# Part of a weight transpose moved out of the first top-k search into an earlier FFN and kept in DRAM; the search's remaining transposes spread evenly; a weighted sum with its operands exchanged

## The chip, the cores and the metric

One core of one Trainium2 chip. The metric is device microseconds of one execution. The engines are PE (TensorE), DVE (VectorE), ACT (ScalarE), POOL (GpSimd) and SP (SyncE), which issues all the DMAs of this kernel.

## The reference

x is 8 x 112 x 256 in float32, the context 8 x 375 x 256. Four layers follow each other, each of the form x = x + tanh(gate) * f(x):

```
x += tanh(g0) * dtw_align(ctx, layernorm(x))           # dynamic time warping, backtracked
x += tanh(f0) * bit_linear(silu(dwconv(bit_linear(layernorm(x), w1))), w2)      # the FFN
x += tanh(g1) * attention(layernorm(x), ctx)           # 16 heads of 16
x += tanh(f1) * neuron_ffn(layernorm(x))
# neuron_ffn(x):
a0 = mean_s(gelu(x @ input_patterns.T))                # 8 x 2048
repr = a0 where a0 is among its row's 256 largest, else 0
a1 = gelu(repr @ process_input_weights.T)              # 8 x 1024, weights 1024 x 2048
w  = softmax(the row's 128 largest of a1);  agg = w @ process_values[chosen]    # 8 x 128
a2 = gelu(agg @ output_input_weights.T)                # 8 x 2048
out = (the row's 256 largest of a2) @ output_patterns[chosen]     # 8 x 256, the same for all s
```

## The kernel before

The whole problem lives on one core. Every engine has one hand-written instruction list. `plan_psum` (L88) deals out the eight PSUM banks in the order in which PE fills them; `claim` (L477) makes PE wait until the bank's last content was drained, `fill` and `drain` count on two semaphores of the bank.

**The FFN** (from about 205 us) works on eight tiles c of 128 hidden units and two halves of 448 tokens. PE: `ffn_up(c, half)` (L1926, product at L1931). DVE: `dequantise` (L1092), then the conv's last tap at L1116 and, each second c, a maximum at L1123 to L1128. ACT: loop L1594 to L1607 (middle tap L1600, left tap L1603, Silu of tile c - 2 at L1607). POOL adds the left tap (L777). The tile buffers `hb` and `ct0` have three slots, so tile c waits for the conv of c - 3. After the loop the scale is transposed and spread (`hmaxT`, `s2bc`, L1957 to L1968), DVE scales and rounds eight tiles, ACT rounds three of them (L1610 to L1614), and PE makes `ffn_down` (L1969 to L1981), whose tile c waits for its rounding. In the FFN SP loads the attention's key stacks (`load_stack`, L593) for batch entries 0, 1, 2 into the three slots of `ks`, and stores and loads split keys (L606, L599). The attention starts at about 284 us, on the first slot.

**The last layer**. PE makes 32 pattern products (L2087) up to about 477 us; beside them SP loads `piw`, two slots of one 128 x 2048 tile of the process weights each (L645 to L648). Then comes a search for the 256 largest of each row (`largest`, L1289): the values lie as 128 lanes of 128, and in each of 2 x 8 rounds DVE counts how many lie below three candidates (L1343), PE adds the counts of a row's lanes (`count`, L2174 to L2186), DVE compares them (L1355) and makes the next candidates (L1361). Into this search the transposes of the process weights are placed (L2206 to L2217): PE does four groups of four 128 x 128 transposes (L2213) for tile i, then two counts, for i = 0 to 7; ACT copies each group from PSUM to `piwT` (L1718). After the ties (L2194, L2195) DVE makes the picked values, PE transposes them (L2203), DVE copies them to `repr32` (L1393), and PE, after 32 waits for the drains of all the groups (L2221 to L2223), starts `process` (L2230).

The second search has 12 rounds of 7 candidates, DVE and ACT sharing the counting. Its result goes to the weighted sum `aggr` (L2256, L2259): for each of 8 tiles the 128 x 128 process values stand as PE's weights and 8 columns of softmax terms pass; then, for the sum of the terms, a matrix of ones stands as weights. DVE takes the reciprocal (L1418) and multiplies (L1420), and PE makes `output` (L2267). A third search, the final product and the write follow.

Of the kernel before, what the change touches and what calls it, by code (L numbers as in the profile page):

```python
# [20 lines left out]
NH, HD = 16, 16  # L21
# [9 lines left out]
UP0 = 3  # L31
ACT_ROUNDS = (1, 3, 5)
# [55 lines left out]
def plan_psum():  # L88
# [42 lines left out]
    for b in range(B):  # L131
        ring(("expand", b))
    for half in range(2):
        for h in range(DH):
            ring(("qxT", h, half))
        ring(("sxbc", half))
        if half == 0:
            for c in range(UP0):
                ring(("ffn_up", c, 0))
    for c in range(HT):  # L140
        for half in range(0 if c >= UP0 else 1, 2):
            ring(("ffn_up", c, half))
    for half in range(2):
        ring(("hmaxT", half))
    p.add("s2bc", 6, 7)
    for pair in range(HB):
        p.add(("ffn_down", pair), pair)
# [35 lines left out]
    for p_ in range(NPT):  # L183
        for m in range(NIT // 4):
            ring(("piwT", p_, m), (0, 1, 2, 3))
    for k in range(3):
# [12 lines left out]
        elif k == 1:  # L199
            p.add("aggr", 2)  # L200
            p.add("output", 3)
# [7 lines left out]
def build_program(nc, x_in, ctx_in, g_xattn, g_ffn, w1_in, conv_w, conv_b, w2_in,  # L209
                  wq_in, bq_in, wk_in, bk_in, wv_in, bv_in, wo_in, bo_in,  # L210
                  pat_in, piw_in, pval_in, oiw_in, opat_in, out, key_parts, keys):
    plan = plan_psum()
    ctx = ExitStack()
    with ctx:
# [81 lines left out]
        last_stack = rk.at - 2 * NH * SC  # L296
        ln0 = Region(rk.at).take("ln0", [S, B, D])
# [131 lines left out]
        agr = r1.take("agr", [128, B])  # L429
# [73 lines left out]

        parts_stored = [sem(f"parts_stored{i}") for i in range(2)]
# [48 lines left out]
        def _(sp):  # L553
# [64 lines left out]
            for b in range(2):  # L618
                store_parts(b)
                load_keys(b + 2)  # L620
            sp.wait_ge(x_ready, B)
            sp.wait_ge(consts_ready, 1)
            for b in range(3):
                sp.dma_start(ks[SR:SR + 3, b, :, :], onesb[0:3, :].unsqueeze(1).broadcast_to([3, NH, SC])
                             ).then_inc(loaded["ones_k"], 16)
            for b in range(2):
                load_stack(b)
            for b in range(2, B):
# [3 lines left out]
                if b == 2:  # L632
                    load_stack(2)
# [11 lines left out]
            for i in range(NPT):  # L645
                if i >= 2:
                    wait_filled(sp, ("piwT", i - 2, NIT // 4 - 1))
                sp.dma_start(piw[:, i % 2, :], piw_in[128 * i:128 * (i + 1), :]).then_inc(loaded[f"piw{i % 2}"], 16)  # L648
# [140 lines left out]
        def _(dve):  # L789
# [644 lines left out]
        def _(act):  # L1434
# [158 lines left out]
            whole_columns(1)  # L1593
            for c in range(HT + 2):  # L1594
# [119 lines left out]
            for i in range(NPT):  # L1714
# [28 lines left out]
        def _(pe):  # L1743
# [191 lines left out]
            for half in range(2):  # L1935
# [32 lines left out]
            fill(ins, "s2bc")  # L1968
            for c in range(HT):  # L1969
# [236 lines left out]
            for i in range(NPT):  # L2206
                pe.wait_ge(loaded[f"piw{i % 2}"], 16 * (i // 2 + 1))
                for m in range(NIT // 4):
                    nm = ("piwT", i, m)
                    claim(pe, nm)  # L2210
                    for e in range(4):
                        c = 4 * m + e
                        ins = tr(bank(nm)[:, 128 * e:128 * e + 128], piw[:, i % 2, 128 * c:128 * c + 128],  # L2213
                                 ident[:, :])
                    fill(ins, nm)
                for r in (2 * i, 2 * i + 1):
                    count(0, r)  # L2217
            ties(0)
            sel_transpose(0)
            wait_drained(pe, ("selT", 0))  # L2220
            for i in range(NPT):  # L2221
                for m in range(NIT // 4):
# [90 lines left out]
```

## Time and profile before

| | |
|---|---|
| three executions | 618.41, 618.11, 621.31 us (median 618.41) |
| the profiled execution | 620.62 us; its span from the first to the last instruction 618.8 us |
| busy | PE 67%, DVE 69%, ACT 46%, POOL 16% |
| mean granted TensorE clock | 0.796 of full speed |

The profile gives for each instruction its line, engine, operands, start and duration, and in square brackets the idle time of its engine before it with what ended it. The granted clock of PE has two levels, 0.50 (1.2 GHz) and 1.00 (2.4 GHz). The chain of waits follows the work that ended last back from the last instruction.

### The profile page before, as it was taken

What the parts mean: (1) busy time and instruction counts of PE and PEld (TensorE: products, weight loads), DVE (VectorE), ACT (ScalarE), POOL (GpSimd) and SP (SyncE); (2) the same over time, 40 slices, a digit from 0 to 9 for tenths busy, and PEclk for the clock granted to TensorE, in tenths of its full rate; (3) what the DMA queues carried; (4) which work ended last, traced back from release to release, by engine and by line L of the source; (5) the groups of instructions that cost most, each with busy time, mean ns of one, the idle gap of its engine ahead of it and who ended that gap; (6) DMA issues with size and microseconds to landing.
All of it is one profiled execution on the core that took longest, in us unless ns stands there. A gap on an engine that the chain in (4) does not pass through costs nothing.

```text
span 618.8 us, 10227 instructions
## 1 busy us (share of the span) xinstructions
PE 415.4 (67%) x3424; PEld 295.1 (48%) x3424; DVE 428.8 (69%) x1711; ACT 284.9 (46%) x657; POOL 97.9 (16%) x235
## 2 busy tenths in 40 slices
PE   3798899732293601856899998999999556207206
PEld 3467686511172301834677776776455552107203
DVE  7645999899938697768788887864534763671673
ACT  3745444812224773444365556654434451450440
POOL 6780000000065462035700000000000000000000
PEclk9997699755576855669699999999999887755556
DMA  9600004194025980000566857600300560000002
GB/s 283 187 1 1 1 2 150 57 210 107 2 78 104 139 141 19 0 0 15 147 116 89 200 82 139 173 1 1 137 1 0 176 234 0 2 1 0 0 1 60
DMA packets 34666, 47.23 MB, mean 76 GB/s; under 512 B 5542, under 2 KB 32055, under 8 KB 32823
## 3 DMA queue, kind: packets, MB, share of 16 engines
q1 hardware_dynamic: 34614, 46.58, 32.2%
q8 instruction: 28, 0.46, 0.3%
q14 instruction: 24, 0.19, 0.1%
HBM read 37.87 MB, written 8.60 MB: 75 GB/s over the span
## 4 chain that ended last, share of the span: by engine, by line
PE 54%; DVE 24%; ACT 11%; issue 6%; POOL 4%; DVEq 0%; POOLq 0%; ACTq 0%
PE ps L2087 7%; PE ps L2041 4%; DVE PR L1028 4%; PE ps L2028 4%; ACT below L1708 4%; PE ps L2017 4%; PE ps L1850 4%; PE ps L1858 3%; PE ps L2003 3%; PE ps L2213 2%; PE ps L1914 2%; DVE prod L1024 2%; DVE below L1343 2%; PE ps L1809 2%; DVE ct L1116 2%
## 5 line engine op out<-in xcount | busy, mean ns | idle before, releaser
L1679 ACT ACTIVATE E<-ps 125x448 f32<-125x448 f32 x96 | 52.1, 543 | 46.3 <-PE ps L2028 46.2
L1215 DVE TENSOR_REDUCE negm<-ps 112x1 f32<-112x375 f32 x128 | 66.0, 544 | 10.6 <-PE ps L2017 7.4
L2186 PE MATMUL ps<-cnt,same 128*128 128x3 bf16 (+4 forms) x40 | 6.8, 170 | 61.6 <-ACT below L1708 41.1
L2017 PE MATMUL ps<-ks,qs 96*112 96x375 bf16 x128 | 44.2, 357 | 2.8 <-ACT qs L1672 2.5
L2041 PE MATMUL ps<-E,v 125*32 125x112 f32 x768 | 42.7, 273 | 0.0
L2028 PE MATMUL ps<-qs,ks 99*125 99x112 bf16 x384 | 40.4, 229 | 1.0 <-ACT E L1679 0.5
L1203 DVE TENSOR_REDUCE acts<-gel 128x4 f32<-128x448 f32 x32 | 19.8, 620 | 29.3 <-ACT gel L1647 29.3
L2028 PEld LDWEIGHTS ps<-qs,ks 99*125 99x125 bf16 x384 | 35.2, 141 | 9.7 <-issue 6.3
L2186 PEld LDWEIGHTS ps<-cnt,same 128*128 128x128 bf16 (+1 forms) x40 | 4.3, 107 | 64.7 <-issue 64.7
L1647 ACT ACTIVATE gel<-ps 128x448 f32<-128x448 f32 x32 | 17.3, 543 | 29.3 <-PE ps L2087 29.3
L1236 DVE CAST qs<-ps 3x448 bf16<-3x448 f32 x32 | 20.1, 630 | 13.4 <-PE ps L2058 13.3
L762 POOL CAST kp<-kx 128x750 bf16<-128x750 f32 x8 | 6.5, 810 | 141.1 <-ACT path L1565 127.7
L1028 DVE TENSOR_TENSOR_SCAN PR<-UU,PR,prod 128x94 bf16<-128x94 bf16 x63 | 26.1, 414 | 2.2
L2003 PE MATMUL ps<-qp,pick 128*96 128x112 bf16 x384 | 25.5, 218 | 2.2 <-issue 2.2
L2003 PEld LDWEIGHTS ps<-qp,pick 128*96 128x96 bf16 x384 | 24.8, 128 | 4.3 <-issue 3.0
L2087 PE MATMUL ps<-ln3Ta,patT 128*128 128x448 f32 x64 | 25.3, 543 | 1.2 <-ACT gel L1647 1.2
L1718 ACT ACTIVATE piwT<-ps 128x512 f32<-128x512 f32 x32 | 17.1, 603 | 16.4 <-PE ps L2213 16.3
L1888 PE MATMUL ps<-lanes_at,turned 64*47 64x32 bf16 x125 | 5.2, 203 | 28.4 <-ACT turned L1557 28.4
L2087 PE MATMUL ps<-ln3Tb,patT 128*128 128x448 f32 x64 | 24.2, 539 | 0.0
L1672 ACT ACTIVATE qs<-ps 96x448 bf16<-96x448 f32 x32 | 17.2, 539 | 14.4 <-PE ps L2003 14.4
L2041 PEld LDWEIGHTS ps<-E,v 125*32 125x32 f32 x768 | 19.6, 109 | 8.5 <-issue 5.5
L2017 PEld LDWEIGHTS ps<-ks,qs 96*112 96x112 bf16 x128 | 16.7, 134 | 14.1 <-issue 8.9
(371 smaller groups left out, 1131.3 us busy)
## 6 DMA issues: line engine op xcount, KB each, us to landing
ks<-key_parts SPq DMA_DIRECT2D x48, 187.5 KB, 6.8
piw<-fn_process_input_weights SPq DMA_DIRECT2D x8, 1024.0 KB, 4.9
key_parts<-kp SPq DMA_DIRECT2D x48, 93.8 KB
ctx_again<-in_ctx SPq DMA_DIRECT2D x7, 512.0 KB
keys<-kx SPq DMA_DIRECT2D x16, 187.5 KB, 2.1
kx<-keys SPq DMA_DIRECT2D x8, 375.0 KB, 6.7
ctxP<-in_ctx SPq DMA_DIRECT2D x8, 256.0 KB, 6.2
patn<-in_L_ffn_input_patterns SPq DMA_DIRECT2D x1, 2048.0 KB, 16.1
```

What stands on the lines that cost most here:

```text
L1028: dve.tensor_tensor_scan(PR[:, t, 2:PW], UU[:, t, 0:2 * RB], prod[:, :], PR[:, t, 1:2], ALU.mult, ALU.add).then_inc(traced, 1)
L1203: dve.tensor_reduce(a0[:, HB * half:HB * half + HB, i % NIT], gel[:, i % 2, :].rearrange("p (b s) -> p b s", b=HB), AX.X, ALU.add).then_in ...
L1215: drain(dve.tensor_reduce(negm[:, n:n + 1], bank(nm)[0:S, 0:SC], AX.X, ALU.max, negate=True), nm)
L1236: drain(dve.tensor_copy(qs[SR:SR + 3, (f + 1) // 4 % 3, n:n + 4, :].rearrange("p n s -> p (n s)"), bank(nm)[SR:SR + 3, 0:4 * S]), nm)
L1679: drain(fn(E[:, (KCH * f + c) % 6, :], bank(nm)[0:KC, 0:4 * S], ACT.Exp), nm)
L1708: ins = fn(below[0:n, m, :], val[0:n, :], ACT.Sign, bias=cand[0:n, m:m + 1], scale=-1.0, accum_out=cnt[0:n, m:m + 1])
L1850: ins = mm(bank(nm)[0:KC, 0:D], ctxT[:, h, b, KC * c:KC * c + KC], wvT[:, h, :], start=(h == 0), stop=(h == DH - 1))
L2003: ins = mm(bank(nm)[0:SR, S * i:S * i + S], pick[:, part, 4 * (u % 2) + i, :], qp[:, tile, part, S * (u // 4):S * (u // 4) + S], start=(pa ...
L2017: fill(mm(bank(nm)[0:S, 0:SC], qs[0:SR, u // 4 % 3, n, :], ks[0:SR, u // 4 % 3, n, :], start=True, stop=True), nm)
L2028: ins = mm(bank(nm)[0:KC, S * i:S * i + S], ks[0:SR + 3, f // 4 % 3, n, KC * c:KC * c + KC], qs[0:SR + 3, f // 4 % 3, n, :], start=True, s ...
L2041: ins = mm(bank(("pv", b))[32 * g:32 * g + 32, S * t:S * t + S], v1[:, c, b, (HD + 1) * n:(HD + 1) * n + 32], E[:, (KCH * f + c) % 6, S * ...
L2087: ins = mm(bank(nm)[:, 0:448], patT[:, h, 128 * (i % NIT):128 * (i % NIT) + 128], ln3T[i // NIT][:, h, :], start=(h == 0), stop=(h == DH - 1))
```

## The change

Process-weight tiles 0, 1, 2 (of 8) are transposed in the FFN. Six blocks of 128 x 1024 (`piwE`, e = 0 to 5) are loaded to `piw_raw` (3 slots), transposed by PE (8 transposes into two banks), copied by ACT to `piw_out` (2 slots) and stored by SP to a new DRAM tensor `piw_t`. Their buffers lie in slots 1 and 2 of `ks`, whose loads come later. The FFN's ring of banks has six banks, not eight. In the last layer three DMAs bring the 3 MB back (`load_turned`), and the search holds the 20 groups of the other five tiles: three ahead of it, then one after nearly each count. The waits for the groups' drains stand ahead of the transpose of the picked values. The weighted sum has the softmax terms (8 columns) as weights and the values (128 columns) and one column of ones pass; its 8 x 128 result is scaled, transposed by PE and copied by DVE.

```diff
@@ plan_psum
+    six = tuple(range(6))
+    n[0] = 0
     for half in range(2):
         for h in range(DH):
-            ring(("qxT", h, half))
+            ring(("qxT", h, half), six)
...
+    for e in range(2 * NE - 1):
+        p.add(("piwE", e), 6, 7)
...
     p.add("s2bc", 6, 7)
+    p.add(("piwE", 2 * NE - 1), 4, 5)
@@ SP, ahead of and in the FFN
-            for b in range(3):
-                (ones of slot b)
-            for b in range(2):
-                load_stack(b)
-            for b in range(2, B):
+            load_ones(0)
+            load_stack(0)
+            for e in range(3):
+                load_raw(e)
+            store_parts(2)
+            load_keys(4)
+            store_parts(3)
+            load_keys(5)
+            for e in range(2 * NE):
+                if e + 3 < 2 * NE:
+                    wait_filled(sp, ("piwE", e))
+                    load_raw(e + 3)
+                wait_drained(sp, ("piwE", e))
+                sp.dma_start(piw_t[8 * (e % 2):8 * (e % 2) + 8, :, 128 * (e // 2):128 * (e // 2) + 128
+                                   ].rearrange("c n p -> n c p"), piw_out[:, e % 2, :, :]
+                             ).then_inc(turned_stored[e % 2], 16)
+            for i in range(2):
+                sp.wait_ge(turned_stored[i], 16 * NE)
+            for b in range(1, 3):
+                load_ones(b)
+            for b in range(1, 3):
+                load_stack(b)
+            for b in range(4, B):
@@ SP, last layer
+            load_turned(0, 5)
+            load_turned(12, NIT)
+            for i in range(NE, NPT):
+                j = i - NE
+                if j == 2:
+                    wait_filled(sp, ("pattern", 2 * NIT - 1))
+                    load_turned(5, 12)
+                if j >= 2:
                     wait_filled(sp, ("piwT", i - 2, NIT // 4 - 1))
+                sp.dma_start(piw[:, j % 2, :], piw_in[128 * i:128 * (i + 1), :]).then_inc(loaded[f"piw{j % 2}"], 16)
@@ ACT, in the FFN's loop over c (after the Silu of c - 2) and after it
+            def keep_turned(e, at):
+                nm = ("piwE", e)
+                wait_filled(act, nm)
+                if e >= 2:
+                    act.wait_ge(turned_stored[e % 2], 16 * (e // 2))
+                drain(fn(piw_out[:, e % 2, :, :]..., psum[:, at:at + 2, :], ACT.Copy), nm)
...
+                if 0 <= c - 3 < 2 * NE - 1:
+                    keep_turned(c - 3, 6)
             load_table(ACT.Sqrt)
+            keep_turned(2 * NE - 1, 4)
@@ PE, in the FFN
+            def early_turn(e, at):
+                nm = ("piwE", e)
+                claim(pe, nm)
+                pe.wait_ge(raw_loaded[e % 3], 16 * (e // 3 + 1))
+                for k in range(8):
+                    ins = tr(psum[:, at + k // 4, 128 * (k % 4):128 * (k % 4) + 128],
+                             piw_raw[:, e % 3, 128 * k:128 * k + 128], ident[:, :])
+                fill(ins, nm)
             for c in range(HT):
                 for half in range(0 if c >= UP0 else 1, 2):
                     ffn_up(c, half)
+                if 0 <= c - 3 < 2 * NE - 1:
+                    early_turn(c - 3, 6)
...
             fill(ins, "s2bc")
+            early_turn(2 * NE - 1, 4)
@@ PE, first search
+            turns = (NPT - NE) * (NIT // 4)
+            lead = 3
+            for g in range(lead):
+                turn_weights(g)
+            for r in range(2 * ROUNDS[0]):
+                count(0, r)
+                share = [lead + (turns - lead) * q // (2 * ROUNDS[0]) for q in (r, r + 1)]
+                for g in range(*share):
+                    turn_weights(g)
+            ties(0)
+            pe.wait_ge(turned_loaded, 48)
+            for i in range(NE, NPT):
                 for m in range(NIT // 4):
+                    wait_drained(pe, ("piwT", i, m))
             sel_transpose(0)
             wait_drained(pe, ("selT", 0))
-            for i in range(NPT):
-                for m in range(NIT // 4):
-                    wait_drained(pe, ("piwT", i, m))
@@ PE, weighted sum (the waits for pval and oiwT now stand ahead of sel_transpose(1))
             for i in range(NPT):
-                mm(bank("aggr")[:, 0:B], pval[:, i, :], cells(esel, NPT)[:, :, i], start=(i == 0),
-                   stop=(i == NPT - 1))
-            for i in range(NPT):
-                ins = mm(bank("aggr")[:, B:2 * B], ones[:, :], cells(esel, NPT)[:, :, i], start=(i == 0),
+                mm(bank("aggr")[0:B, 0:DPV], cells(esel, NPT)[:, :, i], pval[:, i, :], start=(i == 0), stop=False)
+                ins = mm(bank("aggr")[0:B, DPV:DPV + 1], cells(esel, NPT)[:, :, i], ones[:, 0:1], start=False,
                          stop=(i == NPT - 1))
             fill(ins, "aggr")
+            claim(pe, "aggT")
+            wait_drained(pe, "aggr")
+            fill(tr(bank("aggT")[:, 0:B], agg8[:, :], ident[0:B, 0:B]), "aggT")
@@ DVE, weighted sum
-            did(dve.reciprocal(agr[:, :], bank("aggr")[:, B:2 * B]))
+            did(dve.reciprocal(agr[:, :], bank("aggr")[0:B, DPV:DPV + 1]))
             settle()
-            drain(tt(agg[:, :], bank("aggr")[:, 0:B], agr[:, :], ALU.mult), "aggr")
+            drain(ts(agg8[:, :], bank("aggr")[0:B, 0:DPV], agr[:, 0:1], None, ALU.mult), "aggr")
+            wait_filled(dve, "aggT")
+            drain(dve.tensor_copy(agg[:, :], bank("aggT")[:, 0:B]), "aggT")
```

## Rows read from the trace of the kernel before

**Rows 1.** The page's chain that ended last, shares of the span by engine.
```profile
PE 54%; DVE 24%; ACT 11%; issue 6%; POOL 4%; DVEq 0%; POOLq 0%; ACTq 0%
```
**Rows 2.** Timeline of DVE, first search: start us, us, engine line, [idle before <- releaser].
```profile
485.22 0.16 DVE L1355 SCALAR_TENSOR_TENSOR reached<-ps,most 128x3 f32<-128x3 f32 x1 [0.21 <-PE ps L2186]
...
488.50 0.16 DVE L1355 SCALAR_TENSOR_TENSOR reached<-ps,most 128x3 f32<-128x3 f32 x1 [1.78 <-PE ps L2186]
...
492.14 0.16 DVE L1355 SCALAR_TENSOR_TENSOR reached<-ps,most 128x3 f32<-128x3 f32 x1 [0.43 <-PE ps L2186]
...
505.35 0.16 DVE L1355 SCALAR_TENSOR_TENSOR reached<-ps,most 128x3 f32<-128x3 f32 x1 [1.99 <-PE ps L2186]
```
**Rows 3.** Timeline of PE, first search.
```profile
490.13 1.94 PE L2213 MATMUL ps<-ident,piw 128*128 128x128 f32 x16
...
501.78 3.49 PE L2213 MATMUL ps<-ident,piw 128*128 128x128 f32 x16
...
515.67 0.16 PE L2194 MATMUL ps<-tie,same 128*128 128x1 bf16 x1 [1.37 <-DVE eq L1372]
```
**Rows 4.** Timeline of DVE and PE, from the picked values to the process product.
```profile
517.81 0.29 DVE L1393 COPY repr<-ps 128x128 f32<-128x128 f32 x1 [0.63 <-PE ps L2203]
...
519.25 8.44 PE L2230 MATMUL ps<-piwT,repr 128*32 128x512 f32 x64 [1.48 <-issue]
```
**Rows 5.** Windows: busy of PE, PEld, DVE, ACT, POOL, then granted clock, DMA share, GB/s.
```profile
195.00:213.00 18.00, 10.80 (x60) 7.16 (x60) 11.28 (x28) 12.06 (x20) 3.71 (x3) 0.73 0.97 130
...
488.00:500.00 12.00, 6.76 (x59) 5.96 (x57) 8.96 (x68) 7.11 (x14) 0.00 (x0) 1.00 0.73 262
519.00:522.40 3.40, 3.15 (x20) 0.97 (x24) 0.00 (x0) 0.00 (x0) 0.00 (x0) 0.55 0.00 0
522.40:528.00 5.60, 5.60 (x55) 1.82 (x48) 0.00 (x0) 0.85 (x2) 0.00 (x0) 1.00 0.00 0
560.00:576.00 16.00, 14.62 (x66) 14.14 (x66) 0.59 (x3) 0.37 (x2) 0.00 (x0) 0.50 0.00 0
```
**Rows 6.** Timeline of PE and DVE at the weighted sum, and one PE transpose ahead of it.
```profile
530.20 0.27 PE L2243 MATMUL ps<-ident,pmx 128*8 128x128 f32 x1 [1.07 <-DVE pmx L1403]
...
558.67 0.18 PE L2194 MATMUL ps<-tie,same 64*64 64x1 bf16 x1 [1.34 <-DVE eq L1372]
558.72 0.19 PE L2195 MATMUL ps<-tie,under 64*64 64x1 bf16 x1
...
560.71 3.55 PE L2256 MATMUL ps<-esel,pval 128*128 128x8 f32 x16 [0.36 <-DVE esel L1416]
...
567.71 0.21 DVE L1418 RECIPROCAL agr<-ps 128x8 f32<-128x8 f32 x1 [7.10 <-PE ps L2259]
...
568.22 6.97 PE L2267 MATMUL ps<-agg,oiwT 128*128 128x8 f32 x32 [0.55 <-issue]
```
**Rows 7.** Timeline of ACT, FFN loop; one row of ACT's copies in the first search.
```profile
224.26 1.14 ACT L1600 ACTIVATE ct<-hb,cb,cws 128x896 f32<-128x896 f32 x1 [2.11 <-DVE hb L1099]
...
239.19 0.95 ACT L1607 ACTIVATE hs<-ct 128x896 f32<-128x896 f32 x1 [3.46 <-DVE ct L1116]
...
502.90 0.60 ACT L1718 ACTIVATE piwT<-ps 128x512 f32<-128x512 f32 x1 [2.75 <-PE ps L2213]
```
**Rows 8.** Timeline of PE and ACT, FFN: products in the loop, then the rounding.
```profile
215.28 1.68 PE L1931 MATMUL ps<-qxT,w1T 128*128 128x448 bf16 x4 [5.42 <-DVE hb L1099]
...
252.76 1.04 ACT L1612 ACTIVATE hs<-hs,magic 128x896 f32<-128x896 f32 x1 [11.11 <-DVE hs L1160]
...
253.32 10.06 PE L1978 MATMUL ps<-w2T,q 128*112 128x256 bf16 x64 [2.71 <-DVE q L1156]
```
**Rows 9.** The page's DMA issues: out<-in, count, KB each, median us from issue to landing.
```profile
ks<-key_parts SPq DMA_DIRECT2D x48, 187.5 KB, 6.8
piw<-fn_process_input_weights SPq DMA_DIRECT2D x8, 1024.0 KB, 4.9
...
pval<-in_L_ffn_process_values SPq DMA_DIRECT2D x1, 512.0 KB, 16.7
```

More of the change, by code:

```diff
@@ L31 @@
 UP0 = 3
+NE = 3
 ACT_ROUNDS = (1, 3, 5)
@@ L132, in plan_psum @@
         ring(("expand", b))
+    six = tuple(range(6))
+    n[0] = 0
     for half in range(2):
         for h in range(DH):
-            ring(("qxT", h, half))
-        ring(("sxbc", half))
+            ring(("qxT", h, half), six)
+        ring(("sxbc", half), six)
         if half == 0:
             for c in range(UP0):
-                ring(("ffn_up", c, 0))
+                ring(("ffn_up", c, 0), six)
+    for e in range(2 * NE - 1):
+        p.add(("piwE", e), 6, 7)
     for c in range(HT):
         for half in range(0 if c >= UP0 else 1, 2):
-            ring(("ffn_up", c, half))
+            ring(("ffn_up", c, half), six)
     for half in range(2):
-        ring(("hmaxT", half))
+        ring(("hmaxT", half), six)
     p.add("s2bc", 6, 7)
+    p.add(("piwE", 2 * NE - 1), 4, 5)
     for pair in range(HB):
@@ L182, in plan_psum @@
     n[0] = 0
-    for p_ in range(NPT):
+    for p_ in range(NE, NPT):
         for m in range(NIT // 4):
@@ L210, in build_program @@
                   wq_in, bq_in, wk_in, bk_in, wv_in, bv_in, wo_in, bo_in,
-                  pat_in, piw_in, pval_in, oiw_in, opat_in, out, key_parts, keys):
+                  pat_in, piw_in, pval_in, oiw_in, opat_in, out, key_parts, keys, piw_t):
     plan = plan_psum()
@@ L296, in build_program @@
         last_stack = rk.at - 2 * NH * SC
+        early_raw = Region(rw.at + 2 * NH * SC)
+        piw_raw = early_raw.take("piw_raw", [128, 3, 1024])
+        piw_out = early_raw.take("piw_out", [128, 2, 8, 128])
+        assert early_raw.at <= rk.at
         ln0 = Region(rk.at).take("ln0", [S, B, D])
@@ L428, in build_program @@
         pmd = r1.take("pmd", [B, B])
-        agr = r1.take("agr", [128, B])
+        agr = r1.take("agr", [B, 1])
+        agg8 = r1.take("agg8", [B, DPV])
         agg = r1.take("agg", [128, B])
@@ L502, in build_program @@
              "pmx_ready pmd_ready pexp_ready vec scl pol").split()]
+        raw_loaded = [sem(f"raw_loaded{i}") for i in range(3)]
+        turned_stored = [sem(f"turned_stored{i}") for i in range(2)]
+        turned_loaded = sem("turned_loaded")
         parts_stored = [sem(f"parts_stored{i}") for i in range(2)]
@@ L2205, in _, with turn_weights @@
             act_transpose(0)
-            for i in range(NPT):
-                pe.wait_ge(loaded[f"piw{i % 2}"], 16 * (i // 2 + 1))
-                for m in range(NIT // 4):
[L2209 to L2218, printed above, removed]
+            def turn_weights(g):
+                i, m = NE + g // (NIT // 4), g % (NIT // 4)
+                pe.wait_ge(loaded[f"piw{(i - NE) % 2}"], 16 * ((i - NE) // 2 + 1))
+                nm = ("piwT", i, m)
+                claim(pe, nm)
+                for e in range(4):
+                    c = 4 * m + e
+                    ins = tr(bank(nm)[:, 128 * e:128 * e + 128], piw[:, (i - NE) % 2, 128 * c:128 * c + 128],
+                             ident[:, :])
+                fill(ins, nm)
+            turns = (NPT - NE) * (NIT // 4)
[9 more added lines that the diff above has]
+            pe.wait_ge(turned_loaded, 48)
+            for i in range(NE, NPT):
+                for m in range(NIT // 4):
+                    wait_drained(pe, ("piwT", i, m))
             sel_transpose(0)
             wait_drained(pe, ("selT", 0))
-            for i in range(NPT):
-                for m in range(NIT // 4):
-                    wait_drained(pe, ("piwT", i, m))
             for h in range(2):
@@ L2250, in _ @@
             ties(1)
+            pe.wait_ge(loaded["pval"], 16)
+            for m in range(NOT // 4):
+                wait_drained(pe, ("oiwT", m))
             sel_transpose(1)
```

26 lines of the change are left out of this document (15 added, 11 removed).

## The prediction

> **What bounds the kernel now.** I read the chain of waits first, for which engine sets the end, then the timelines of the stretches that the change touches, then the granted clock there. No engine bounds the kernel: the chain passes from PE (54%) to DVE (24%) to ACT (11%) [rows 1], so each edit is worth what it takes off the chain of its own stretch, and the profile's busy shares say little.
>
> In the first search the chain is DVE's: a round is three counts on DVE, a short PE matmul, a comparison and new candidates. Between the rounds' starts lie 1.71 us where nothing is in the way (483.98 to 485.69 in the timeline), with DVE idle for 0.21 us while PE counts [rows 2]. But every second count stands on PE behind 16 transposes. At the full clock they take 1.94 us, which is longer than the 1.5 us that DVE leaves PE, and DVE waits 0.43 us, not 0.21; at the half clock they take 3.29 us (not shown) or 3.49 us [rows 3], and DVE waits 1.78 and 1.99 us [rows 2]. That is what the even spreading goes for. The reader should then see 1.48 us of "issue" on PE after DVE has long copied the picked values: 32 semaphore waits [rows 4].
>
> In the weighted sum PE is all there is: from 560.71 to 567.67 it passes 8 columns over 128-column weights, 32 times, at the half clock [rows 5, 6]. In the FFN loop no engine is full; ACT has pauses of 2.11 and 3.46 us (and one of 1.36 us at 231.84), PE one of 5.42 us before it has even reached the last products [rows 7, 8].
>
> **The change, part by part.**
>
> *Search, spreading.* A group is four transposes: 0.49 us at the full clock (1.94 / 4), 0.87 us at the half clock (3.49 / 4) [rows 3]. One group after a count fits into DVE's 1.5 us at either clock. What goes is all that DVE waited above 0.21 us: 1.57 + 1.78, and four times 0.22 [rows 2], together **-4.2 us**. Nothing else is late in its place: ACT copies a group in 0.60 us [rows 7]; the load of tile 5 starts after the fourth group, some 8 us ahead of its first transpose, and a load lands in 4.9 us [rows 9], as do tiles 6 and 7 with some 3 us to spare. In the last round there are two groups: at the half clock 1.74 us, where PE has 1.37 us before the ties [rows 3]: **+0.35 us**, nothing at the full clock. I take the half clock, because PE has less to do than before; both earlier drops came beside pauses of PE.
>
> *Search, waits.* DVE's copy ends at 518.10, PE starts at 519.25 [rows 4], 1.15 us later; I leave 0.1 us of that for the hand-over itself. The 21 waits that are left (20 groups, and the returned tiles) pass in 0.7 us (1.05 / 32 each) between the ties and the picked values, which lie 1.65 us apart in the timeline (515.67 to 517.32). **-1.05 us.**
>
> *Loads of the returned 3 MB.* The first two start at 436.8, with 40 us of pattern products ahead of them; the third, 1.4 MB, starts at 477.9 and is wanted at 513. At the 262 GB/s of this stage [rows 5] it takes 5.4 us. No cost, with 30 us of cover.
>
> *Process stage, clock.* The clock is at the half level when the product starts and at the full from 522.40, 3.15 us later [rows 4, 5]. In ffn_down PE is dense from 253.32 and its 64 passes of 256 columns take 10.06 us [rows 8]; at 0.213 us each they would take 13.6, at the full clock half, so the last 3.6 us ran at the full clock and the rise came some 6 us after the start. If the product had to wait as long, it would lose half of the 2.9 us between. I take **+0.5 us**, a third of the way, with 0 and +1.4 as ends.
>
> *Weighted sum.* Before: 6.96 us to 567.67 for 32 passes [rows 6], 0.22 each, set by the load of 128 float32 columns. After: 16 passes of 128 columns over 8-column weights and 16 of one column. A float32 pass of 128 columns takes 0.22 us at the half clock (3.49 / 16 [rows 3]); the two tie matmuls, one column each with their weights changed between them, start 0.05 us apart [rows 6]. So 16 x 0.22 + 16 x 0.05 = 4.3 us, **-2.65 us**; above, if each small one costs as much as a full one, nothing is gained; below, 3.5 us. Added: a PE transpose of the 8 x 128 result, 0.27 us alone [rows 6] and 0.2 us of handing over, and a DVE copy with its hand-over, 0.3 us; DVE's product has 128 columns and not 8, 0.05 us: **+0.8 us**. The five waits moved ahead of the transpose of the picked terms: **-0.1 us**.
>
> The Trainium skill, "TensorE: Matmul & The Clock Gate", Part 3, says that a weight load overlaps running matmuls only in another row group. All weights here use all rows. But 16 transposes with a weight load each, all in the same rows, pass in 1.94 us at 0.12 us each [rows 3]; loads of 0.11 us and passes of 0.12 us one after the other would be 3.7 us. The trace speaks against the rule; it is one of the rivals.
>
> *FFN loop.* ACT gets five copies of 1024 columns. A 512-column copy takes 0.60 us, an 896-column Silu 0.95 [rows 7]: 1.05 us on that line. I laid the loop out with these durations (ACT 1.13, 0.95, 0.93 a tile; DVE 0.54 for a half tile, 1.05 for the conv, 2.05 and 1.08 for a maximum; POOL 2.0 and never beside DVE's two-input operations, as 211.45 in the timeline shows, where the conv took 3.02 and not 1.14 us). Before and after differ by **1.05 us**: four copies fall into ACT's pauses, and one shows, as PE's tile 6 comes 1.3 us late behind the third block (226.2 and not 224.9). PE cannot turn block e before ACT has kept block e - 1, and tile e + 4 stands behind it; this is the new wait, and DVE waits for it. At the ends: 0 if PE's clock is high and pauses suffice, 5.3 if nothing is covered.
>
> *After the loop.* The sixth block is turned from 250.6 to 252.3, in PE's pause of 2.71 us [rows 8], and kept by ACT to 253.4; ACT's first rounding started at 252.76 and is two times 1.04 us [rows 8], so PE's second tile of ffn_down has to wait until 255.6 and not 255.05: **+0.55 us**. PE is what bounds ffn_down (64 passes in 10.06 us), so it stays.
>
> *SP and DMA in the FFN.* The first slot's six loads come in 1.125 MB; at the 130 GB/s of a full queue [rows 5] they are in at about 203, block 0 behind them at about 206. PE wants it at 208 and could wait until 214 before tile 4 is late (its pause of 5.42 us [rows 8]). Blocks 3 to 5 are asked for two tiles ahead, and 512 KB is half of what lands in 4.9 us [rows 9]. ACT's third copy needs the first store landed: issued at 220, wanted at 227. SP stands in its waits until about 257, then loads slots 1 and 2 (2.25 MB, 17 us at 130 GB/s) to about 277; slot 1 is read at about 293. Behind SP's waits nothing is queued that is wanted before POOL's keys at 290. No cost; the cover is 15 us for slot 1.
>
> **The sum**: -4.2 + 0.35 - 1.05 + 0.5 - 2.65 + 0.8 - 0.1 + 1.05 + 0.55 = -4.75 us. The profiled execution took 620.6 us, the median is 618.4, so this is 615.9 against its own time and **613.7 us** against the median.
>
> **The rivals.**
>
> *A, the FFN covers nothing.* All six copies (6.3 us) and the late rounding show: instead of +1.6 it is +6.3, and the time is 618.4. Against it are 7 us of ACT's pauses; for it, that the pauses are where ACT waits for DVE, and DVE would then wait for PE. 0.11.
>
> *B, slower: the ring of stores.* Block e + 2 can be kept only when store e has landed. Two such periods lie between the first copy and the fifth, 17 us in the layout. A store of 512-byte rows might land as late as the 512 KB of 512-byte rows of pval did, 16.7 us [rows 9]; two of them are 33 us, and the FFN takes 16 us longer: 629. It decides from about 11 us a store on (2 x 11 - 17 = the 5 us gained). For it is that the rows are as short; against it, that pval stood behind 2 MB of another load and these stand behind 0.5 MB. 0.04.
>
> *C, the sum's passes gain nothing.* If each weight load waits for the pass ahead of it, each of the 16 wide passes costs as one alone, 0.27 us [rows 6], and each load and small pass 0.18: 7.2 us and not 4.3, and the stage is 1 us slower than before. Time 616.6. 0.07. It is the rule quoted above.
>
> *D, a clock gift.* The sum's wide passes bring PE to the full clock: `output` takes 6.97 us at the half clock [rows 6], and at the full one half of that; 3.4 us less, 610.3. Against it: PE was over 90% busy from 560 to 576 and stayed at 0.50 [rows 5], though with 8 columns a pass; and the sum is but 4.3 us long. 0.10. That transposes keep the clock up here is plain: from 488 to 500 PE did nothing but transposes and 3-column counts, and was granted 1.00 [rows 5].
>
> The same page, Part 4, says that in transpose mode the full clock does not engage. The trace disagrees, as that row shows. By the rule the search would run at the half clock, which costs the 0.35 us that the sum already holds.
>
> **The numbers.** Forecast 0.68, A 0.11, B 0.04, C 0.07, D 0.10. The range: below, the gifts of D less part of the costs; above, C, or a FFN with half of A: 610.5 to 617.2. About 0.5% (3.1 us) is what a measurement of this kernel tells from no change. Faster by more needs under 615.3: nearly all of the forecast and D, so 0.78. Within: the forecast's upper tail, C, A, so 0.17. Slower: 0.05.
>
> **What the profile should show.** DVE idle before L1355 0.21 us in all rounds of the first search, its rounds 28.3 us together and not 32.6; PE's process product 0.1 us behind DVE's copy; the sum 4.3 us from first pass to last; the stretch from the FFN loop's first product (205.5) to the maximum's transposes (243.4) 1 us longer than its 37.9; ffn_down's second tile waiting for ACT. The forecast fails if the FFN has grown by over 3 us, if PE waits for a raw block or ACT for a store, if slots 1 or 2 of the key stacks are late at 293 us, or if the sum's passes are 0.4 us each.

## The result, and where the time went

In paired runs on one chip the changed kernel takes 612.5 us (611.3 to 612.9, 4 runs) and the kernel before 619.9 (618.1 to 621.5, 4 runs): a ratio of 0.986, 95% interval 0.982 to 0.990. Run again (`after_again`), 612.1 against 620.0, 0.986 (0.982 to 0.990). The forecast was 613.7 us, in a range of 610.5 to 617.2, with 0.78 on faster.

The sum said -4.75 us, and the paired medians differ by 7.4 us. The forecast's 613.7 comes near to 612.5 in part because it starts from a median of 618.4 us, where the paired median of the kernel before is 619.9. The profiled executions differ by 7.7 us (620.6 and 612.9; spans 618.8 and 611.0). So the sum was right in sign and range, and not in each term. These are lines of the page of the kernel after: its busy times, its chain by engine and its DMA issues.

```profile
PE 420.8 (69%) x3425; PEld 291.9 (48%) x3425; DVE 430.6 (70%) x1712; ACT 284.7 (47%) x651; POOL 95.6 (16%) x235
...
PE 51%; DVE 25%; ACT 13%; issue 6%; POOL 4%; DVEq 0%; ACTq 0%; POOLq 0%
...
piw<-fn_process_input_weights SPq DMA_DIRECT2D x5, 1024.0 KB, 5.1
...
piw_raw<-fn_process_input_weights SPq DMA_DIRECT2D x6, 512.0 KB, 8.3
piw_t<-piw_out SPq DMA_DIRECT2D x6, 512.0 KB, 3.2
```

The chain still passes between engines, as in [rows 1], so the time must be read stage by stage. A stage here runs from the start of one instruction on the chain to the start of the next, in the timelines. Two executions of each kernel are shown (`before_again` is the kernel before, unchanged).

| stage, us | before | before_again | after | after_again |
|---|---|---|---|---|
| start to the FFN loop's first product | 205.54 | 204.42 | 204.89 | 204.86 |
| to the maximum's transposes | 37.85 | 37.68 | 40.49 | 40.41 |
| to ffn_down (two stages) | 9.93 | 9.93 | 9.93 | 9.93 |
| ffn_down to DVE's first x | 9.44 | 9.24 | 8.94 | 9.48 |
| x to the attention's first product | 21.40 | 21.31 | 21.97 | 21.44 |
| to the first search | 198.10 | 196.99 | 197.48 | 197.13 |
| first search to the transpose of picked values | 35.06 | 35.98 | 31.21 | 31.21 |
| that transpose to the process product | 1.93 | 1.93 | 0.83 | 0.83 |
| process product to its last transposes | 9.24 | 9.28 | 10.62 | 10.53 |
| second search | 32.22 | 32.27 | 32.26 | 32.29 |
| weighted sum to the output product | 7.51 | 7.51 | 5.12 | 5.06 |
| output product to its transpose | 7.42 | 7.43 | 5.68 | 5.73 |
| third search to the final product | 30.06 | 30.05 | 30.05 | 30.06 |
| final product to the end | 13.13 | 13.05 | 11.52 | 11.45 |

From the first to the third column: -0.65 at the start, **+2.64** in the FFN loop, -0.50 + 0.57 after it, -0.62 in and before the attention, **-3.85** in the search, **-1.10** behind it, **+1.38** in the process product, **-2.39** in the sum, **-1.74** in the output product and **-1.61** at the end; with the small rest -7.8 us. The last two no term of the forecast held.

**The search** is as it was drawn. DVE's comparisons (timeline of DVE, kernel after) wait 0.21 us in 14 rounds, where [rows 2] has up to 1.99, and 0.35 in the last of each half:

```profile
484.93 0.16 DVE L1408 SCALAR_TENSOR_TENSOR reached<-ps,most 128x3 f32<-128x3 f32 x1 [0.21 <-PE ps L2267]
...
488.35 0.16 DVE L1408 SCALAR_TENSOR_TENSOR reached<-ps,most 128x3 f32<-128x3 f32 x1 [0.21 <-PE ps L2267]
...
496.90 0.16 DVE L1408 SCALAR_TENSOR_TENSOR reached<-ps,most 128x3 f32<-128x3 f32 x1 [0.35 <-PE ps L2267]
...
511.53 0.16 DVE L1408 SCALAR_TENSOR_TENSOR reached<-ps,most 128x3 f32<-128x3 f32 x1 [0.35 <-PE ps L2267]
```

In PE's timeline one group of four transposes stands behind each count, two behind the last. The process product starts 0.06 us after DVE's copy ends (515.67), not 1.15 [rows 4], and it is 9.80 us long where it was 8.44. The sum's 32 passes (its 16 float32 products stand as two each in the trace) end after 3.85 us, two wide and two narrow ones together 0.47 us; then come PE's transpose and the output product:

```profile
493.40 1.09 PE L2295 MATMUL ps<-ident,piw 128*128 128x128 f32 x4
...
511.45 1.94 PE L2295 MATMUL ps<-ident,piw 128*128 128x128 f32 x8
...
515.73 9.80 PE L2321 MATMUL ps<-piwT,repr 128*32 128x512 f32 x64 [0.38 <-DVE repr L1446]
...
558.61 0.59 PE L2349 MATMUL ps<-pval,esel 128*8 128x128 f32 x2 [0.41 <-DVE esel L1469]
558.99 0.24 PE L2350 MATMUL ps<-ones,esel 128*8 128x1 f32 x2
559.09 0.58 PE L2349 MATMUL ps<-pval,esel 128*8 128x128 f32 x2
...
563.18 0.20 PE L2355 MATMUL ps<-ident,agg 8*128 8x8 f32 x1 [0.71 <-DVE agg L1473]
563.73 5.23 PE L2359 MATMUL ps<-agg,oiwT 128*128 128x8 f32 x32 [0.35 <-DVE agg L1475]
...
603.76 3.68 PE L2380 MATMUL ps<-fin,batch_of 128*112 128x256 f32 x16 [0.64 <-DVE fin L1481]
```

**The clock** explains the terms beside these. Windows of the kernel after (columns as in [rows 5]):

```profile
488.00:500.00 12.00, 8.07 (x34) 5.65 (x35) 9.51 (x75) 3.58 (x6) 0.00 (x0) 0.50 0.38 141
515.70:521.50 5.80, 5.77 (x32) 1.36 (x35) 0.00 (x0) 0.00 (x0) 0.00 (x0) 0.52 0.00 0
521.50:526.00 4.50, 4.50 (x44) 1.36 (x36) 0.00 (x0) 0.99 (x2) 0.00 (x0) 1.00 0.00 0
558.60:562.00 3.40, 3.39 (x29) 2.32 (x30) 0.00 (x0) 0.00 (x0) 0.00 (x0) 0.50 0.00 0
562.50:566.00 3.50, 2.47 (x20) 2.44 (x21) 0.66 (x3) 0.00 (x0) 0.00 (x0) 0.95 0.00 0
599.50:603.00 3.50, 3.50 (x32) 1.36 (x32) 0.00 (x0) 0.00 (x0) 0.00 (x0) 0.50 0.02 5
603.40:607.00 3.60, 3.24 (x15) 2.73 (x16) 2.76 (x7) 0.00 (x0) 0.00 (x0) 1.00 0.25 71
```

The spread search runs at the half clock from 487.1 on, where the old one ran at the full from 488 to 500 [rows 5]. The process product then has its first 5.5 us at the half clock, and had 2.8 before: the windows give rises at 521.3 and, in the kernel before, at 522.05, not at the 522.40 that the prediction read (its window from 519.00 to 522.40 has a mean of 0.55 [rows 5], which holds 0.34 us at the full clock). That the slower search makes this rise late is not shown: turn_later, below, has the same search at the half clock, and there the rise came 3.7 us after the product's start. The next rise comes at 562.2, just before the sum's last pass ends, and the full clock lasts until 565.6, so it covers the output product's first 1.9 us. The last stage's spreading product (L2380) comes wholly after the rise. In the kernel before the clock rose 8.5 us after the final product's start, and the same 16 matmuls took 5.78 us (timeline of PE, kernel before):

```profile
605.67 3.64 PE L2281 MATMUL ps<-opat,repr 128*32 128x256 f32 x32 [0.38 <-DVE repr L1424]
609.96 5.78 PE L2288 MATMUL ps<-fin,batch_of 128*112 128x256 f32 x16 [0.64 <-DVE fin L1426]
```

### The profile page after: what moved, and what is told of

The parts are those of the page before. It is cut to its first block, busy times and chain, and to the rows that moved or that the text cites. A ratio compares the mean times of both kernels' runs of the same rounds, so it can differ in the third digit from the quotient of the medians.

```text
span 611.0 us, 10254 instructions
## 1 busy us (share of the span) xinstructions
PE 420.8 (69%) x3425; PEld 291.9 (48%) x3425; DVE 430.6 (70%) x1712; ACT 284.7 (47%) x651; POOL 95.6 (16%) x235
## 4 chain that ended last, share of the span: by engine, by line
PE 51%; DVE 25%; ACT 13%; issue 6%; POOL 4%; DVEq 0%; ACTq 0%; POOLq 0%
PE ps L2168 7%; PE ps L2122 4%; DVE PR L1081 4%; PE ps L2109 4%; ACT below L1775 4%; PE ps L2098 4%; PE ps L1917 4%; PE ps L1925 3%; PE ps L2084 3%; DVE below L1396 3%; PE ps L1981 2%; DVE prod L1077 2%; PE ps L1876 2%; PE ps L2321 2%; PE ps L2072 1%
## 5 line engine op out<-in xcount | busy, mean ns | idle before, releaser
L1917 PE MATMUL ps<-wvT,ctxT 128*125 128x256 f32 x96 | 22.2, 395 | 0.0
```

The source lines that it names most:

```text
L1917: ins = mm(bank(nm)[0:KC, 0:D], ctxT[:, h, b, KC * c:KC * c + KC], wvT[:, h, :], start=(h == 0), stop=(h == DH - 1))
```

## The experiments

Ten runs on three chips, two of them repeats of the kernels before and after and one of spread8_four. Each stands beside the kernel before on its chip (medians 620.6, 620.0 and 620.5 us). The stages of eight, in us (`four_2` is spread8_four_again):

| stage | turn_later | after_burst | wsum_only | spread8_two | spread8_four | four_2 | warm | warmer |
|---|---|---|---|---|---|---|---|---|
| FFN loop | 37.80 | 40.46 | 37.83 | 37.69 | 37.65 | 37.72 | 37.74 | 37.68 |
| first search | 31.21 | 33.91 | 38.16 | 34.40 | 31.57 | 31.73 | 31.26 | 31.28 |
| to process | 0.83 | 0.83 | 1.91 | 0.69 | 0.69 | 0.69 | 0.69 | 0.68 |
| process | 9.67 | 9.37 | 9.28 | 7.88 | 9.57 | 9.58 | 7.88 | 7.88 |
| second search | 32.29 | 32.31 | 32.29 | 32.30 | 32.30 | 32.26 | 32.24 | 33.43 |
| sum | 5.26 | 5.23 | 5.24 | 5.24 | 4.95 | 5.12 | 5.23 | 3.55 |
| output | 7.42 | 7.43 | 7.42 | 7.42 | 5.88 | 5.70 | 7.43 | 6.13 |
| final to end | 11.51 | 11.47 | 13.10 | 11.24 | 11.21 | 11.19 | 11.32 | 9.73 |
| median us | 608.5 | 617.0 | 616.2 | 612.0 | 608.9 | 609.3 | 607.8 | 606.3 |

### turn_later: where the FFN's 2.6 us come from

The changed kernel, with each block's transposes one tile later on PE.

```diff
-                if 0 <= c - 3 < 2 * NE - 1:
-                    early_turn(c - 3, 6)
+                if 0 <= c - 4 < 2 * NE - 1:
+                    early_turn(c - 4, 6)
+            early_turn(2 * NE - 2, 6)
```

> The changed kernel, but on PE each early block's transposes stand one tile later, behind ffn_up of tile e + 4 and not ahead of it; ACT is unchanged. Theory 1 (the 2.6 us that the FFN loop lost come from PE's late tile 6, which lets DVE's conv of tile 4 lose the port to POOL's add): the stretch from the loop's first product (L1998, x10) to the maximum's transposes is within 0.8 us of the 37.9 us before, not 40.5 us, and the kernel is about 2 us faster than the change, 610 to 611 us. Rival (ACT's five copies themselves are what shows, 0.5 us each): the stretch stays at 40.5 us or more and the time at 612.5. Second rival (the copies now come later and ACT holds up tile 7): 39 to 41 us with ACT's copy ahead of DVE's wait in the timeline.

Measured: 608.5 us (607.1 to 609.1, 6 runs), ratio 0.980 (0.977 to 0.983), 12 us under the kernel before. The loop is back at 37.80 us with all five of ACT's copies in it, 1.00 us each. So the copies cost nothing; PE's order did. In the changed kernel block 2 stands on PE ahead of tile 6, and waits for ACT's copy of block 1; DVE's dequantising waits for tile 6 (timeline of the kernel after, DVE, POOL and DVE):

```profile
225.12 1.16 DVE L1152 TENSOR_TENSOR hb<-ps,sxbc 128x448 f32<-128x448 f32 x2 [0.57 <-PE ps L1998]
225.82 2.09 POOL L830 TENSOR_TENSOR ct<-ct,hs 128x896 f32<-128x896 f32 x1 [2.46 <-ACT hs L1667]
226.20 2.66 DVE L1169 SCALAR_TENSOR_TENSOR ct<-hb,cws,ct 128x896 f32<-128x896 f32 x1
...
230.87 1.86 DVE L1181 TENSOR_TENSOR hmax<-hmax,hmax 128x896 f32<-128x896 f32 x1
```

The 0.57 us are small. But DVE's conv (L1169) now starts after POOL's addition and not before it, and takes 2.66 us instead of 1.14; later the maximum (L1181) takes 1.86 instead of 1.09. In turn_later DVE is first by 0.06 us, and POOL is the one that is slowed (same view):

```profile
224.44 1.14 DVE L1169 SCALAR_TENSOR_TENSOR ct<-hb,cws,ct 128x896 f32<-128x896 f32 x1
224.50 3.05 POOL L830 TENSOR_TENSOR ct<-ct,hs 128x896 f32<-128x896 f32 x1 [2.45 <-ACT hs L1667]
...
227.59 1.09 DVE L1181 TENSOR_TENSOR hmax<-hmax,hmax 128x896 f32<-128x896 f32 x1
```

In the kernel before DVE is first by the same 0.06 us (226.49 and 226.55). In after_again it is later by 0.12 (225.83 and 225.71), and its conv takes 2.92. In the kernel after the wait (0.57), the longer conv (1.52) and the longer maximum (0.77) add up to 2.9 us, against the loop's 2.6. So PE's order is worth 2.6 us of a loop, as the run shows; that it acts through this race is read from the traces.

### wsum_only: the weighted sum by itself

The kernel before with the diff's parts for the weighted sum on PE and DVE, and the five waits ahead of the transpose of the picked terms. Nothing else.

> The kernel before with nothing but the weighted sum turned round and its five waits moved. Expected from the trace of the change: from the sum's first pass to output's first pass 5.1 us, not 7.5, so 2.4 us faster than before. output itself took 5.2 and not 7.0 us in the change since the clock rose for 3.4 us in it. Theory (the sum's wide passes bring the rise): it is here too, 4.1 us faster than before in all. Rival (chance of where the clock's change falls): output takes 7.0 us again, 2.4 us faster than before.

Measured: 616.2 us (614.0 to 621.7, 12 runs), ratio 0.9935 (0.991 to 0.996). From sum to output it is 5.24 us, 2.27 less than before, at a clock of 0.50, so rival C is out: it would have left the stage 1 us slower. The ratio says 4 us, not 2.3, and the rest is in the last stage: the spreading product takes 3.68 us here and 5.78 in the kernel before (the table's 13.10 includes a last write that landed after 3.9 us in this one execution, where the others took about 2). So the 4.1 us of the expectation's theory came out by another path than its own. The output product took 7.42 us, with no rise, as its rival said.

### spread8_two and spread8_four: is DRAM needed?

All 32 groups spread over the search of the kernel before, four of them ahead of it, with the turned sum and the moved waits, and nothing in the FFN. spread8_two keeps the two load slots; spread8_four adds two, in memory that patterns have left by then:

```diff
+        piw_more = Region(loads.at).take("piw_more", [128, 2, NI])
-                if i >= 2:
-                    wait_filled(sp, ("piwT", i - 2, NIT // 4 - 1))
-                sp.dma_start(piw[:, i % 2, :], ...)
+                if i >= 4:
+                    wait_filled(sp, ("piwT", i - 4, NIT // 4 - 1))
+                sp.dma_start(piw_slot(i), ...)
```

> The same with the two load slots of the kernel before. A tile's groups now take some 3.9 us and a load lands in 4.9 us, so tile i + 2 cannot be there when tile i + 1 is done: about 1 us of stall for each of six tiles, in front of a count. Expected: search rounds 32 to 35 us together, no faster than the search before, PE waiting for piw; the time 3 to 6 us above the four-slot kernel. Rival (loads land in time, as 5.3 us lay between a tile's end and the next but one before): equal to the four-slot kernel.

> The kernel before with the weighted sum and the moved waits of the change, and with all 32 groups of transposes spread over the first search (four ahead, then one or two after a count); no early transposes, no DRAM; the process weights have four load slots, two of them where the input patterns lay. Theory (what gained in the search is the even spreading, and with four slots the loads don't stand in its way): the 16 rounds of the search take 28.3 us if PE's clock stays high (two groups are 0.98 us, DVE leaves 1.5), the FFN loop stays at 37.9 us, and the kernel is about 2 us faster than the change, near 610. If the clock falls, two groups take 1.74 us and each such round 0.25 us more: search 31 us, near 613. Rival (moving three tiles out is what makes the spreading possible): search rounds of 2 us and more, time above the change's.

Measured: two slots 612.0 us (610.9 to 613.8, 4 runs), ratio 0.986 (0.982 to 0.990); four slots 608.9 us (608.0 to 612.7, 6 runs), 0.982 (0.978 to 0.986), and on another chip 0.982 (0.980 to 0.984). On the chip of the first two turn_later took 608.5 us. With two slots PE reaches tiles before their loads (timeline of PE, spread8_two, two of four such waits), and the search takes 34.40 us:

```profile
504.29 0.66 PE L2221 MATMUL ps<-ident,piw 128*128 128x128 f32 x4 [1.05 <-DMA piw<-fn_process_input_weights]
...
509.71 1.97 PE L2221 MATMUL ps<-ident,piw 128*128 128x128 f32 x8 [1.30 <-DMA piw<-fn_process_input_weights]
```

With four it takes 31.57, 0.36 us more than with three tiles moved out, and the FFN is untouched. The move through DRAM, 3 MB each way and six blocks in another layer, buys 0.4 us that four slots do not; what had to be hidden was a load. The two searches did not have the same clock: with four slots 21 of the 31.6 us were at the full clock, with the tiles moved out 3.5 (after) and 5.0 (turn_later) of 31.2. A round with two groups at the half clock keeps DVE 0.2 us longer (0.44 and 0.43 against 0.21), so at the half clock throughout the four slots would cost more; no run shows how much.

### after_burst: the spreading alone

The changed kernel, but with its five tiles in bursts of 16 transposes ahead of every second of the first ten counts.

> The changed kernel with the five tiles of the search left in bursts as before: 16 transposes ahead of every second count of the first ten, nothing after; three tiles still go through DRAM. Theory (the even spreading is what gains in the search, moving the tiles out is not): each of the four bursts behind a count still costs DVE 0.2 us at the full clock and 1.6 to 1.9 us at the half clock; the clock tends to fall with so little work, so search to transpose of the picked values takes 33 to 38 us, not 31.2, and the kernel is 2 to 5 us slower than the change. Rival (with 12 groups gone the search is free of PE in any order): 31.5 to 32 us and the change's time.

Measured: 617.0 us (614.2 to 617.7, 11 runs), ratio 0.993 (0.991 to 0.996), and 4.8 us more than after_again on the same chip. The search is 2.7 us longer than spread. The output product is 1.7 us longer, without the early rise, and the process product's stage 1.2 us shorter, as the clock rose 3.0 us after its start and not 5.4. Of the five bursts two meet the half clock (timeline of DVE, after_burst):

```profile
490.18 0.16 DVE L1408 SCALAR_TENSOR_TENSOR reached<-ps,most 128x3 f32<-128x3 f32 x1 [1.43 <-PE ps L2267]
...
495.25 0.16 DVE L1408 SCALAR_TENSOR_TENSOR reached<-ps,most 128x3 f32<-128x3 f32 x1 [1.86 <-PE ps L2267]
```

What a burst costs hangs on the clock it meets: the old layout's search took 35.1, 36.0 and 38.2 us in three traces (before, before_again, wsum_only), the spread one 31.2 in all three of after, after_again and turn_later.

### warm and warmer: buying the clock

spread8_four with filler products between the counts, whose results nothing reads. In warm 1 after each of the last six counts of the first search and 3 behind its ties, and 5 or 2 after the later counts of the other two; in warmer up to 8 there.

```diff
+            def keep_warm(k, n):
+                wait_drained(pe, ("actT", k))
+                for _ in range(n):
+                    mm(bank(("selT", k))[:, 128:128 + SC], identb[:, :], onesb[:, 0:SC], start=True, stop=True)
...
                 count(0, r)
+                if r >= 10:
+                    keep_warm(0, 1)
```

> The four-slot kernel with matmuls added whose results nobody reads (375 columns, into free columns of a bank): one after each of the last six counts of the first search, five after most of the last counts of the other two, two or three after the ties. They lie in PE's idle time. Theory (what is left in the process product, the sum, output and the final products is PE's half clock, and activity ahead of them raises it): process 7 us and not 9.6, sum and output 6 us and not 10.8, final product and spreading 2 us less; 5 to 9 us faster than the four-slot kernel, near 602. Rival (the added matmuls push counts back, or the clock falls in the short waits anyway): the four-slot kernel's time or a little more.

> The kernel with all eight tiles spread and four load slots, with filler products in all three searches: as in the one-search version for the first, and in the second and third 8 after each count from the sixth to the ninth, 5 and 7 in the later ones and 5 after the ties. The fillers' results are read by nothing. Theory (the clock is lost for want of products on PE and kept by them, and the stages after a search are PE's): the granted clock stays at 1.00 from about 488 us to the end of the searches, the chain from attention's transpose to the output product's end falls from 12.8 us to about 9, the spreading product of the last stage by 2 us more, and the time is 602 to 604.5 us. Rival (the fillers themselves push the counts back: eight of 375 columns take 1.25 us at full and 2.5 us at half clock against a gap of 1.9 us between two counts): the second and third searches grow by 0.6 us for each such count where the clock is half, and the time is 608 us or more.

Measured: warm 607.8 us (605.5 to 611.2, 6 runs), ratio 0.979 (0.975 to 0.983). That is not clear of spread8_four's 0.982 (0.978 to 0.986), and the theory's 602 was missed. The clock stays at 1.00 from 487.6 to 525.1 and the process product's stage takes 7.88 us, so its cost in the changed kernel was the clock. spread8_two, without fillers, has the same 7.88 us, as there the clock had risen at 513.8, before the product. In the second search of warm the clock rose at 545.6 and fell again at 552.4, before the sum. warmer took 606.3 us (603.5 to 607.8, 4 runs), 0.977 (0.973 to 0.980), beside 609.3 of four_2 on the same chip. Its windows and PE's timeline:

```profile
485.70:523.30 37.60, 24.80 (x191) 14.72 (x189) 22.42 (x155) 16.27 (x31) 0.00 (x0) 1.00 0.23 83
523.30:543.70 20.40, 6.94 (x27) 3.35 (x28) 14.86 (x117) 10.13 (x48) 0.00 (x0) 0.51 0.00 1
543.70:557.40 13.70, 10.76 (x87) 7.09 (x85) 6.83 (x47) 4.02 (x14) 0.00 (x0) 0.99 0.01 2
```

```profile
537.97 2.69 PE L2217 MATMUL ps<-onesb,identb 128*128 128x375 bf16 x8
540.59 0.21 PE L2194 MATMUL ps<-cnt,same 64*64 64x7 bf16 x1
...
552.15 0.38 PE L2287 MATMUL ps<-pval,esel 128*8 128x128 f32 x2 [0.41 <-DVE esel L1422]
...
552.42 0.38 PE L2287 MATMUL ps<-pval,esel 128*8 128x128 f32 x2
```

Theory and rival both hold in part, and in the middle they cancel. The sum's pairs take 0.27 us and not 0.47, sum and output together 9.68 and not 10.82, and the end 9.73 and not 11.19. But where the fillers meet the half clock, eight take 2.69 us; two counts then follow after 2.7 and not 2.1 us, and the second search is 1.2 us longer. What stays is the process product's 1.7 and the end's 1.5 us. The theory's 602 to 604.5 us was not reached by the median, nor was its full clock through all searches: it was 0.51 from 523.3 to 543.7.

### The repeats

> The changed kernel unaltered, on the chip and in the call of the others: 612 to 613 us. Its second trace shows which of the parts below repeat and which are the clock's phase: the FFN loop should again take 40.5 us and the search 31.2 us (both set by the order of work); output (5.7 us in the first trace, 7.4 before) and the process product (10.6, 9.2 before) may come out either way if they are the clock's phase.

> The kernel before unaltered, for a second trace of it. If the bursts make its search hang on the clock's phase, search to transpose of the picked values is not 35.1 us again but anything from 32.5 (all bursts at the full clock) to 41 us (all seven at the half clock); the FFN loop should be 37.9 us again and the weighted sum with its handing over 7.5 us.

> The same kernel as spread8_four once more, on the chip of the other one: 607.5 to 609.5 us if chips agree, the first search 31.2 to 31.6 us, and no stretch of full clock in the second and third searches.

after_again: 612.1 us (612.0 to 613.9, 5 runs); before_again: 618.9 us in its one run; spread8_four_again: 609.3 us (608.3 to 609.8, 4 runs). The stages repeat within 0.2 us where no clock boundary or DMA lies in them. Of the ten traces with the turned sum, warmer has the full clock from before it. Of the other nine, four (after, after_again, spread8_four, four_2) have a rise 3.2 to 3.6 us after the sum's first pass, near its end, and so 3.4 us of full clock, of which the output product has 1.7 to 1.9. The other five have none. So the sum alone does not bring it: wsum_only has the same sum and not the rise.

## Why the prediction was right, and where it was not

- **Search, spreading (-4.2 + 0.35):** measured -3.85, the same, against the trace that the forecast was read from; in two other traces of the old layout the search was 36.0 and 38.2 us long, and the gain would have been 4.8 and 7.0. The half clock that I took for the two groups in the last round was there, and held from 487.1 on.
- **Waits (-1.05):** -1.10. The loads of the returned 3 MB were never waited for.
- **Process clock (+0.5, ends 0 and +1.4):** +1.38, at the upper end. The step "a third of the way" had nothing behind it. The row that I had, ffn_down's rise some 6 us after a dense start [rows 8], was the nearest for this kernel: 5.5 and 5.4 us in its two traces. But it is no rule: in turn_later, with the same search and product, the rise came after 3.7 us and the stage took 9.67, +0.43, close to what the forecast took. What sets the moment of the rise was not found.
- **Weighted sum (-2.65 + 0.8 - 0.1):** -2.39 against -1.95. The passes took 3.85 us, not 4.3: two wide and two narrow ones 0.47 us, where I had 0.54. Rival C failed: in the window from 558.60 to 562.00 PE's products were busy for 3.39 of 3.40 us and its 30 weight loads for 2.32 us, so the loads lay beside products. The Trainium skill, "TensorE: Matmul & The Clock Gate", Part 3, lets a load overlap only with products in another row group; all of these use all rows, so the trace disagrees, as it did for the transposes [rows 3]. In its text on the mechanism the same Part of the Trainium skill also lets a load for the background weight buffer go ahead of running products, and with that the trace does not disagree.
- **FFN loop (+1.05):** +2.64, the step that failed. I laid it out, found the wait ("PE's tile 6 comes 1.3 us late behind the third block"), and priced its knock-on with the layout's own times. That the conv and POOL's addition slow each other was right, but the layout's times were not good to 0.06 us, and that is the margin by which one of the two goes first, so that the conv takes 1.14 or 2.66 us. That one of ACT's copies shows was wrong: turn_later has every copy and loses nothing.
- **After the loop (+0.55):** the second tile does wait for ACT, until 257.41, 2.1 us behind the first product, where 2.3 was drawn (255.6 against 253.32) and 1.7 without the change. The stage is -0.50 and +0.04, as the clock rose within it at 258.4 or 261.2 (259.2 before), so the term's size cannot be read from it.
- **SP and DMA:** as drawn. Stores landed in 3.2 us (rival B needed 11), blocks in 8.3, and the stacks' later loads, asked for at 261.8, were not waited for.
- **Not forecast:** -1.74 in the output product, of which rival D spoke (-3.4, chance 0.10) with the reason that the sum would bring the clock up. Here the rise did come in the sum, but gave only 1.9 us of the output product the full clock, and in wsum_only the same sum passed without it, so D's reason is not enough. And -1.6 at the end.

Without these two the spans would differ by 4.4 us, close to the forecast's 4.75, but through errors of both signs: 1.6 us too little for the FFN loop and 0.9 for the process product's clock, against 1.05 too much for ffn_down, 0.4 us too little credited to the sum, and 0.7 us less in stages that the change does not touch. That the total came near was luck.

The Trainium skill, "TensorE: Matmul & The Clock Gate", Part 4, says that the full clock does not engage in transpose mode. In the first search of warmer PE's transposes ran at 1.00 from 485.7 on, as the window from 485.70 to 523.30 shows. Fillers stand among the later ones, so the cleaner row against that statement is still the one from 488 to 500 in the kernel before, which has none [rows 5].

**What stays open.** The early rise in the last stage: all ten traces with the turned sum have the spreading product at 3.68 us, the two without it at 5.78 and 5.74. In nine of the ten the clock rose 3.3 to 4.3 us after the final product's start (warmer had it before), in the other two 8.5 us after. But for warmer, all have the same stretch of 30.1 us with the third search ahead of the final product. That the sum causes this is not shown. A rival is that the moment of a rise does not hang on the final product alone, and that the time saved before it shifts the product to a better place against that moment; two traces of the kernel before are too few to tell, and no run separates the two.

## What to carry to other kernels

Before moving work to another stage to spread what is left, ask what stopped it from being spread where it stands; here it was having only two load slots, and two more gave nearly the same search without the move. Put an inserted step behind the product that the slower engines wait for, not ahead of it: the order alone was worth 2.6 us. And when a hand layout is used for a difference, first see that it reproduces the trace of before; where two engines that slow each other start within 0.1 us, price both orders.

## What the hardware showed that was not expected

- DVE's conv (two float32 inputs of 896 columns) takes 2.92 us when it starts 0.12 us behind a POOL addition and 2.66 when 0.38 us behind; one that starts 0.06 us ahead of it takes 1.14, and POOL's addition takes 3.05 instead of 2.09.
- Float32 passes of 128 columns over 8-column weights and one-column passes, with the weights changed each time, take 0.47 us for two of each at the half clock and 0.27 at the full.
- With eight products of 375 bf16 columns after each later count of the second search the clock rose at 543.5, where without them (four_2) it stayed at 0.50 up to the sum; they cost 0.6 us a round until it had risen. In the first search of all eight tiles one filler after each of the last six counts and three behind the ties went with 1.00 for 37.6 us, where spread8_four had 6.8 us of 0.50 from 496.0 and 3.4 from 513.1.
- The process product, the same in all kernels, had no fixed time at the half clock: 2.8 (before), 2.9 (before_again and wsum_only), 3.0 (after_burst), 3.4 (both of spread8_four), 3.7 (turn_later), 5.4 (after_again) and 5.5 us (after), and none in three traces. Its stage took 9.24 to 10.62 us in the same order, and 7.88 where there was none.
